# Folding the output weight early and spreading its projection over the last half batches of a cross attention kernel

## The chip, the cores and the metric

One core of a Trainium2 chip runs the whole program. The metric is the device time of one execution in microseconds. The engines are TensorE (PE; PEld is its weight load), VectorE (DVE), ScalarE (ACT), GpSimd (POOL) and SyncE (SP), which here only issues DMAs. PE accumulates in eight banks of PSUM; everything else lies in SBUF or, as scratch, in DRAM.

## What is computed

16 sequences of 112 queries attend to 375 context tokens each. There are 32 query heads and 8 key and value heads of width 32; all in float32.

```python
lin = lambda x, W, A, B: x @ W + 2.0 * (x @ A @ B)      # A, B: rank 16
q = lin(x, Wq, Aq, Bq)                                  # 1792 rows x 1024
k, v = lin(ctx, Wk, Ak, Bk), lin(ctx, Wv, Av, Bv)       # 6000 rows x 256
p = softmax(q @ k.T / sqrt(32))                         # per head, 4 query heads share one k, v
out = x + lin(p @ v, Wo, Ao, Bo)
```

## The kernel before

Each weight is folded once: W + 2AB is built block by block, one block being 128 rows of 1024. PE makes the product (`fold`, L706: two matmuls of 512 columns), DVE adds the raw weight (`block_sum`, L1149), ACT rounds the sum to a high part (`block_hi`, L976), and DVE (even blocks) or POOL (odd blocks) subtracts for the low part (`block_lo`, L1169; `pool_lo`, L637). Before a weight's first block its factor A is loaded, copied four times by DVE (`ab_place`, L1127), turned by PE (`turn_a`, L696, eight transposes) and split by ACT and DVE (`ab_hi`, L965; `ab_lo`, L1134). A product of split numbers is three matmuls (`mm3`, L689: L691, L692 and L693).

The query phase goes over 4 groups of 4 sequences. A group has 8 chunks (`q_chunk`, L741), called (g, c) here, of 8 k steps with three matmuls of 448 columns; ACT and DVE drain a chunk (`q_hi`, `q_lo`) and SP stores each pair of chunks (`store_q`, L490; two DMAs) to a scratch. ACT may overwrite a pair's buffer when the store of the pair two before has landed. A chunk needs the drain of the chunk two before. SP issues its DMAs in one written order: ahead of group 1 these are the first context (1.5 MB), then Ao in eight small loads and Bo in four (L435, L444), then the x of group 2 (L470).

The loop then takes one sequence ("batch") per step, in two halves of 4 key heads. A half of batch b holds the score matmuls of b (S, 12 of them, each followed by ACT's exponential and, from the fifth on, one of POOL's eight sums), the maxima of batch b+1 (N, 16 matmuls on two banks, each reduced by DVE, L1268; M turns them), the values or keys of later batches (V, T, K), and at the end the product with the values (P, 24 matmuls, L897) and the denominators (8, L932). `half_order` (L82) lays these out for every engine alike: the dense pieces stand in a row and set the clock with their `COST`, and each item of `PLAN` is put in where its due time, a share of the half, has come. `run_steps` (L390) says which kinds each half has.

The output weight comes last. Its factor is turned ahead of batch 0, where the second score matmul waits for it (L868). Its eight blocks are folded in the second half of batch 14 and the first half of batch 15 (W). Tile 0 of the output (14 tiles of 128 rows, each 2 x 8 x 3 matmuls of 512 columns, `o_piece`, L923) follows the blocks (O, in both halves of batch 15), tile 1 comes in the last half (Z). A tile's input is loaded from a scratch with its inverse denominators (`load_attn`, L563: one DMA and four of `load_inv`), multiplied by DVE (`normalise`, L1288), rounded by ACT (`split`, L1083) and split by DVE (L1294); DVE adds the residual (`add_residual`, L1299) and ACT stores the tile. Tiles 2 to 13 run behind the loop (`tile`, L942). Ahead of the loop ACT waits for all stores of queries (L1097), since the buffers of the output weight overlay theirs.

## Time and profile before

| | us |
|---|---|
| median of 3 runs (1038.49 to 1043.4) | 1040.0 |
| the profiled execution | 1043.98 |
| its span, first to last instruction | 1042.1 |
| PE busy in the span | 972.3 |
| DVE / ACT / POOL busy | 583.6 / 433.5 / 320.1 |

PE is busy when a matmul is in flight; busy is not the same as fast, since the granted clock has two levels (1.2 and 2.4 GHz), and the profile gives the mean granted share (PEclk) of a stretch. An idle time is put down to the instruction that ended it.

### The profile page before, as it was taken

The page shows a single profiled execution, that of the slowest core. Times are in us where ns is not written, and L with a number is a line of the kernel's source. Part 1 is how long each engine was busy: PE and PEld are TensorE (multiplying, and loading weights), DVE is VectorE, ACT ScalarE, POOL GpSimd, SP SyncE. Part 2 cuts the span into 40 slices and gives each one's busy share as a digit, 9 for nine tenths or more (in the row PEclk, how much of TensorE's full clock was granted, in tenths as well). Part 3 has the DMA queues.
Part 4 walks back from the last instruction along what each step waited for, and adds up shares of the span by engine and source line. Part 5 has one row for each costly group of instructions (what it writes and reads, how often), then busy time and mean ns, then how long its engine had stood idle before and what let it go on. Part 6 is the DMA issues. An engine that isn't in the chain of part 4 may idle for free.

```text
span 1042.1 us, 15943 instructions
## 1 busy us (share of the span) xinstructions
PE 972.3 (93%) x5904; PEld 802.1 (77%) x5904; DVE 583.6 (56%) x1005; ACT 433.5 (42%) x843; POOL 320.1 (31%) x276
## 2 busy tenths in 40 slices
PE   6989999977999999999999999999999767989998
PEld 4879999966887887887887877877878534768886
DVE  5661312257577676676677677667667643334321
ACT  3341211223555555555565565555655433201000
POOL 1201000000354354453453553553543545300000
PEclk9999999989899999999999999999999767989999
DMA  6739422643143443444344344245253442477652
GB/s 188 233 92 249 150 97 86 170 101 103 48 111 84 101 111 92 94 111 106 80 110 111 75 111 120 65 112 127 58 123 76 112 130 57 128 222 203 202 158 81
DMA packets 106004, 124.73 MB, mean 120 GB/s; under 512 B 30048, under 2 KB 89568, under 8 KB 105936
## 3 DMA queue, kind: packets, MB, share of 16 engines
q1 hardware_dynamic: 102076, 110.16, 41.3%
q10 hardware_dynamic: 3860, 13.67, 3.6%
q8 instruction: 42, 0.69, 0.3%
q14 instruction: 26, 0.21, 0.1%
HBM read 87.59 MB, written 29.82 MB: 113 GB/s over the span
## 4 chain that ended last, share of the span: by engine, by line
PE 74%; DVE 12%; DMA 5%; ACT 3%; issue 3%; SPq 1%; POOL 0%; ACTq 0%; DVEq 0%; POOLq 0%
PE ps L691 10%; PE ps L692 10%; PE ps L693 10%; PE ps L882 8%; PE ps L897 8%; PE ps L870 7%; PE ps L831 5%; PE ps L833 4%; PE ps L835 4%; PE ps L776 4%; DVE maxima L1268 4%; DVE k_stack L1197 3%; DMA q_scratch<-q_out_lo 3%; PE ps L932 2%; DMA out_dram<-residual 1%
## 5 line engine op out<-in xcount | busy, mean ns | idle before, releaser
L1268 DVE TENSOR_REDUCE maxima<-ps 112x1 f32<-112x375 f32 x512 | 269.2, 542 | 79.8 <-PE ps L882 71.2
L1060 ACT ACTIVATE probs<-ps 125x448 f32<-125x448 f32 x384 | 207.9, 543 | 170.1 <-PE ps L870 169.1
L671 POOL TENSOR_TENSOR prob_sum<-probs 125x448 f32<-125x448 f32 x128 | 146.0, 1156 | 343.4 <-ACT probs L1060 341.9
L882 PE MATMUL ps<-k_stack,q_stack 96*112 96x376 f32 x512 | 185.7, 363 | 21.9 <-DVE maxima L1268 20.3
L870 PE MATMUL ps<-q_stack,k_stack 97*125 97x448 f32 x384 | 146.8, 383 | 12.1 <-DVE a_stack_o L1146 4.3
L677 POOL TENSOR_TENSOR prob_sum<-prob_sum,probs 125x448 f32<-125x448 f32 x128 | 147.4, 1159 | 26.4 <-ACT probs L1060 24.9
L882 PEld LDWEIGHTS ps<-k_stack,q_stack 96*112 96x112 f32 x512 | 92.0, 180 | 46.1 <-DVE maxima L1268 42.0
L831 PE MATMUL ps<-wv_hi,ct_hi 128*125 128x256 f32 x384 | 112.6, 293 | 5.2 <-DVE k_stack L1197 5.2
L833 PE MATMUL ps<-wv_lo,ct_hi 128*125 128x256 f32 x384 | 109.4, 285 | 0.0
L835 PE MATMUL ps<-wv_hi,ct_lo 128*125 128x256 f32 x384 | 109.4, 285 | 0.0
L1191 DVE TENSOR_TENSOR ct_lo<-ps,ct_hi 128x375 fp32r<-128x375 f32 x128 | 70.2, 548 | 55.3 <-ACT ct_hi L997 55.3
L691 PE MATMUL ps<-xt_hi,wq_hi 128*128 128x448 f32 x256 | 97.4, 381 | 1.1 <-DVE wq_lo L1175 0.8
L693 PE MATMUL ps<-xt_hi,wq_lo 128*128 128x448 f32 x256 | 93.9, 367 | 0.0
L692 PE MATMUL ps<-xt_lo,wq_hi 128*128 128x448 f32 x256 | 93.9, 367 | 0.0
L691 PE MATMUL ps<-wo_hi,attn_hi 128*128 128x512 f32 x224 | 89.3, 399 | 3.9 <-DVE attn_lo L1296 3.9
L1197 DVE TENSOR_TENSOR k_stack<-ps,k_stack 32x376 fp32r<-32x376 f32 x128 | 70.0, 547 | 39.7 <-ACT k_stack L1003 36.7
L691 PE MATMUL ps<-ct_hi,wk_hi 128*128 128x376 f32 x256 | 90.7, 354 | 0.3 <-DVE ct_lo L1191 0.3
L693 PE MATMUL ps<-wo_hi,attn_lo 128*128 128x512 f32 x224 | 88.7, 396 | 0.0
L692 PE MATMUL ps<-wo_lo,attn_hi 128*128 128x512 f32 x224 | 88.7, 396 | 0.0
L897 PE MATMUL ps<-probs,v 125*32 125x448 f32 x768 | 82.6, 565 | 5.0 <-ACT probs L1060 4.9
L831 PEld LDWEIGHTS ps<-wv_hi,ct_hi 128*125 128x125 f32 x384 | 73.7, 192 | 17.0 <-DVE k_stack L1197 15.7
L692 PE MATMUL ps<-ct_lo,wk_hi 128*128 128x376 f32 x256 | 86.2, 337 | 0.0
(80 smaller groups left out, 1436.4 us busy)
## 6 DMA issues: line engine op xcount, KB each, us to landing
ctx_in<-in_ctx_dram SPq DMA_DIRECT2D x16, 1344.0 KB
q_stack<-q_scratch SPq DMA_DIRECT2D x96, 224.0 KB, 4.2
x_in<-in_x_dram SPq DMA_DIRECT2D x8, 896.0 KB, 8.7
q_scratch<-q_out_hi SPq DMA_DIRECT2D x16, 448.0 KB, 2.8
q_scratch<-q_out_lo SPq DMA_DIRECT2D x16, 448.0 KB, 3.7
attn_scratch<-attn SPq DMA_DIRECT2D x32, 224.0 KB, 4.1
attn_rows<-attn_scratch SPq DMA_DIRECT2D x14, 512.0 KB, 4.8
inv_tile<-inv_scratch SPq DMA_DIRECT2D x56, 128.0 KB, 5.1
```

Source lines behind the costliest of these rows:

```text
L677: pool.tensor_tensor(prob_sum[:, j, :], prob_sum[:, j, :], probs[:, 2, j, :], ALU.add).then_inc(psum_added, 1)
L691: pe.matmul(dst, l_hi, r_hi, start=start, stop=False)
L692: pe.matmul(dst, l_hi, r_lo, start=False, stop=False)
L693: return pe.matmul(dst, l_lo, r_hi, start=False, stop=stop)
L831: pe.matmul(dst, ct_hi[:, k, rows], wv_hi[:, k, :], start=(k == 0 and i != 1), stop=False, skip_group_check=True)
L833: pe.matmul(dst, ct_hi[:, k, rows], wv_lo[:, k, :], start=False, stop=False, skip_group_check=True)
L835: mm = pe.matmul(dst, ct_lo[:, k, rows], wv_hi[:, k, :], start=False, stop=(k == KC - 1), skip_group_check=True)
L870: pe.matmul(ps[0:TR, score_bank(i), 0:QH], kst[cur][0:STM, g, c * TR:(c + 1) * TR], qst[cur][0:STM, g, :], start=True, stop=True).then_inc ...
L882: mm = pe.matmul(ps[0:NQ, NAT + i % 2, 0:NTE], qst[nxt][0:STK, g, rr * NQ:(rr + 1) * NQ], kst[nxt][0:STK, g, :], start=True, stop=True)
L897: mm = pe.matmul(ps[HD * j:HD * (j + 1), CTX, 0:QH], v_sb[cur][:, c, g * HD:(g + 1) * HD], probs[:, c, j, :], start=(c == 0), stop=(c == T ...
L1060: act.activation(probs[:, c, j, :], ps[0:TR, score_bank(i), 0:QH], ACT.Exp, scale=SM).then_inc(exp_done, 1)
L1268: dve.tensor_reduce(maxima[:, h, i:i + 1], ps[0:NQ, NAT + i % 2, 0:NT], AX.X, ALU.max).then_inc(max_done, 1)
```

## The change

The output weight is folded in the query phase: its factor is turned in chunk (1, 2), and one block is folded in every second chunk from (1, 4) to (3, 2). The blocks use the staging buffers of the other weights; the high part overwrites the raw block, the low part the sum, and SP stores both to a new scratch in DRAM. The two halves of the weight's columns come back in batches 13 (left) and 14 (right). Six pieces of 24 matmuls each, one half of a tile's columns, stand in the last three half batches: the left halves of tiles 0 and 1, the right halves of tiles 0 and 1, then both halves of tile 2. Tiles 3 to 13 follow the loop. X is a tile's normalisation and Y its split. SP takes over the last denominators and the store of tiles 0 and 1, and ACT's wait for the stored queries is gone. Loops over registers are written out. Below is the core of the diff; the rest places buffers and renames arguments.

```diff
+EARLY = [(0, 0, VA), (1, 0, VB), (0, 1, TURN), (1, 1, VA), (2, 0, VB), (2, 1, TURN)]
+EARLY_TILES = 3
+LAST_PIECE = [2, 3, 5]
...
+O_TURN = (1, 2)
+O_FOLDS = {(1, 4): 0, (1, 6): 1, (2, 0): 2, (2, 2): 3, (2, 4): 4, (2, 6): 5, (3, 0): 6, (3, 2): 7}
+WO_KEEP = 7
...
-        "W": 2 * BANK, "O": 6 * BANK, "Z": 3 * BANK}
...
+EXTRA = {"U": [("X", 0, 0.35), ("Y", 0, 0.5)], "O0": [("X", 1, 0.25), ("Y", 1, 0.3)],
+         "O1": [("X", 2, 0.2), ("Y", 2, 0.6)], "O2": [("X", 3, 0.2), ("Y", 3, 0.45)]}
...
-    for name, first in (("W0", 0), ("W1", 4), ("W2", 8)):
-        if name in has:
-            for n in range(first, first + 4 if name != "W2" else KC + OLAG):
...
+    for n in range(HALVES + 1):
+        if f"O{n}" in has:
+            dense += [("O", p, k) for p in (2 * n, 2 * n + 1) for k in range(KC)]
...
-                return wo_hi[:, n, :], wo_lo[:, n, :]
+                return raw1[n % 2][:, :].bitcast(F32R), wsum1[n % 2][:, :].bitcast(F32R)
...
-            wo_factors()
...
-            step(B // 2 - 2, 1, (full[0], full[1] - {"C"}))
-            step(B // 2 - 1, 0, ({"A", "D", "V", "N"}, {"A", "D", "G", "N", "W0"}))
-            step(B // 2 - 1, 1, ({"A", "D", "W1"}, {"A", "D", "G", "W2"}))
+            step(B // 2 - 2, 1, (full[0] | {"L"}, (full[1] | {"L"}) - {"C"}))
+            step(B // 2 - 1, 0, ({"A", "D", "V", "N", "U"}, {"A", "D", "G", "N", "O0"}))
+            step(B // 2 - 1, 1, ({"A", "D", "O1"}, {"A", "D", "G", "O2"}))
...
+            return LAST_PIECE[t] + 1 if t < EARLY_TILES else 2 * t + 2
...
+                if w == W_O and n >= 2:
+                    sp.wait_ge(wo_stored[n % 2], 32 * (n // 2))
+                elif g >= 2:
                     sp.wait_ge(w_summed, g - 1)
...
+            def store_wo(n):
+                wait_lo(sp, QKV_BLOCKS + n)
+                for hl, t in enumerate((raw1, wsum1)):
+                    sp.dma_start(wo_scr[hl, n, :, :], t[n % 2][:, :]).then_inc(wo_stored[n % 2], 16)
+
+            def rows_q(g, n):
+                if (g, 2 * n) in O_FOLDS:
+                    block = O_FOLDS[g, 2 * n]
+                    store_wo(block)
+                    if block + 2 < KC:
+                        load_raw(W_O, block + 2)
+                store_q(g, n)
...
-            with sp.Fori(1, GROUPS - 1) as g:
+            for n in range(2):
+                load_raw(W_O, n)
+            for g in range(1, GROUPS - 1):
                 next_x(g)
                 for n in range(QS):
-                    store_q(g, n)
+                    rows_q(g, n)
             for n in range(QS - 1):
-                store_q(GROUPS - 1, n)
+                rows_q(GROUPS - 1, n)
...
+            def load_left(k):
+
+                for hl in range(2):
+                    to = wo0[hl][:, k, :] if k < WO_KEEP else wo0_end[hl][:, :]
+                    sp.dma_start(to.bitcast(F32), wo_scr[hl, k, :, 0:BANK]).then_inc(wo0_in, 16)
...
+            def load_right(hl):
+
+                for n in range(KC // 2):
+                    sp.dma_start(wo1[hl][:, 2 * n:2 * n + 2, :].bitcast(F32),
+                                 wo_scr[hl, 2 * n:2 * n + 2, :, BANK:H].rearrange("k p n -> p k n")
+                                 ).then_inc(wo1_in[n], 16)
...
-                    if "W0" in has[h]:
-                        load_attn(0, 0)
-                    if "W1" in has[h]:
-                        sp.wait_ge(st_done, NS * 2 * (B - 1))
-                        load_attn(0, 1)
-                        load_residual(sp, 0, 1)
+                    if "U" in has[h]:
+                        load_attn(0)
+                        sp.wait_ge(k_done, 2 * B)
+                        load_right(0)
...
-                        elif kind == "W" and i + 1 in range(2, KC):
-                            load_raw(W_O, i + 1)
-                        elif kind == "Z" and (i, k) == (0, 0):
-                            load_attn(1, 0)
+                        elif kind == "S" and i % 3 == 2 and "L" in has[h]:
+                            sp.wait_ge(st_done, NS * (2 * b + h) + i + 1)
+                            load_left(h * KC // 2 + i // 3)
+                        elif kind == "S" and i == 0 and "O0" in has[h]:
+                            sp.wait_ge(v_done, 2 * B)
+                            load_attn(1)
+                            load_residual(sp, 0)
+                            load_right(1)
+                            load_attn(2)
+                        elif kind == "S" and i == NS - 1 and "O0" in has[h]:
+                            sp.wait_ge(st_done, NS * 2 * (B - 1))
+                            load_residual(sp, 1)
+                        elif kind == "S" and i == 1 and "O1" in has[h]:
+                            load_attn(3)
+                        elif kind == "S" and i == 1 and "O2" in has[h]:
+                            for t in range(2):
+                                store_tile(sp, t)
+                                load_residual(sp, t + 2)
+                            load_attn(4)
...
+            run_steps(sp, step, second_queries)
             store_attn(B - 1, 1)
-            sp.wait_ge(st_done, NS * 2 * B)
-            load_residual(sp, 0, 0)
-            for h in range(HALVES):
-                sp.wait_ge(attn_stored[h], 16 * B)
-            sp.wait_ge(inv_stored, 16 * (B - 1))
-            with sp.Fori(2, OT // 2 - 1) as pair:
-                for par in range(2):
-                    load_attn(pair, par)
-            load_attn(OT // 2 - 1, 0)
-            sp.wait_ge(inv_stored, 16 * B)
-            load_attn(OT // 2 - 1, 1)
+            store_den(sp, 2 * B - 1, B - 1, 1)
+            load_attn(5)
+            load_attn(6)
+            sp.wait_ge(den_stored, 16 * 2 * B)
+            load_den(sp, B - 1)
+            load_attn(7)
+            store_inv(sp, B - 1)
+            for t in range(8, OT):
+                load_attn(t)
...
-            for n in range(1, KC, 2):
-                pool_lo(0, n)
+            for w in (0, W_O):
+                for n in range(1, KC, 2):
+                    pool_lo(w, n)
             wait_qkv(pool)
+            for par in range(2):
+                pool.wait_ge(wo_stored[par], 32 * KC // 2)
...
                 for c in range(2 * RH):
-                    q_chunk(g, c)
...
+                    if (g, c) == O_TURN:
+                        q_chunk(g, c, {KC // 2: lambda: turn_a(W_O, FOLD)})
+                    elif (g, c) in O_FOLDS:
+                        q_chunk(g, c, {KC // 2: lambda n=O_FOLDS[g, c]: fold(W_O, n, FOLD)})
+                    else:
+                        q_chunk(g, c)
+                if g < GROUPS - 1:
+                    pe.wait_ge(q_lo_set, g * 2 * RH + 2 * RH - 1)
...
-                            if i == S_IN_DEN[0] and isinstance(n, int) and n == 0:
-                                pe.wait_ge(a_lo, W_O + 1)
...
                         elif kind == "O":
-                            if i == 0:
...
+                            t, side, bank = EARLY[i]
+                            if k == 0:
+                                pe.wait_ge(at_lo_set, t + 1)
+                                if i < 2:
+                                    pe.wait_ge(v_set, 2 * B)
+                                    pe.wait_ge(wo0_in, 2 * KC * 16)
+                                elif i == 2:
+                                    pe.wait_ge(k_lo_set, NKV * B)
+                                else:
+                                    pe.wait_ge(o_added, i - 2)
+                            if i == 2 and k % 2 == 0:
+                                pe.wait_ge(wo1_in[k // 2], 32)
+                            mm = o_piece(t % 2, side, k, bank)
                             if k == KC - 1:
...
                 for m in range(2):
-                    if isinstance(pair, int) and par == 0:
+                    if t == EARLY_TILES:
+                        pe.wait_ge(o_added, 2 * t + m - 2)
+                    elif t == EARLY_TILES + 1:
                         pe.wait_ge(attn_set, 2 * B)
                         pe.wait_ge(den_copied, 2 * B)
                     else:
                         pe.wait_ge(o_added, 2 * t + m - 3)
                     for k in range(KC):
-                        mm = o_piece(par, m, k, OUT[par])
...
+            for t in range(EARLY_TILES, OT):
+                tile(t)
...
+                    if (g, c) == O_TURN:
+                        ab_hi(W_O, FOLD)
+                    if (g, c) in O_FOLDS:
+                        block_hi(W_O, O_FOLDS[g, c])
...
-            for par in range(2):
-                act.wait_ge(q_stored[par], GROUPS * QS // 2 * 32)
-            run_steps(act, step, lambda: None, wo_factors)
+                if t >= 2:
+                    act.wait_ge(o_done, added(t - 2))
+                if t == 1:
+                    act.wait_ge(v_done, 2 * B)
+                act.activation(at_hi[t % 2][:, :, :], at_raw[t % 2][:, :, :], ACT.Copy).then_inc(at_hi_set, 1)
+
+            run_steps(act, step, lambda: None)
...
-            store_den(act, 2 * B - 1, B - 1, 1)
-            split(1, 1)
...
-            act.wait_ge(inv_set, B - 1)
-            load_den(act, B - 1)
-            store_inv(act, B - 1)
...
-                    load_residual(act, pair, par)
-            for par in range(2):
-                store_tile(OT // 2 - 1, par)
+            for t in range(EARLY_TILES + 1, OT):
+                split(t)
+                store_tile(act, t - 2)
+                load_residual(act, t)
...
+                if w == W_O and n >= 2:
+                    dve.wait_ge(wo_stored[n % 2], 32 * (n // 2))
...
+                    if (g, c) == O_TURN:
+                        ab_lo(W_O, FOLD)
+                    if (g, c) in O_FOLDS:
+                        block_sum(W_O, O_FOLDS[g, c], FOLD)
+                        block_lo(W_O, O_FOLDS[g, c])
                     q_lo(g, c)
-                for k in range(KC):
-                    x_lo(g + 1, k)
-                q_lo(g, 2 * RH - 1)
-            for c in range(2 * RH - 1):
-                q_lo(GROUPS - 1, c)
+                    if (g, c) == (1, 0):
+                        ab_place(W_O)
...
-            ab_place(W_O)
...
-                        elif kind == "W":
-                            block_sum(W_O, i, FOLD_O)
-                            if i % 2 == 1:
...
+                        elif kind == "X":
+                            normalise(i)
+                        elif kind == "Y":
+                            split(i)
+                        elif kind == "S" and i == 2 and "O1" in has[h]:
+                            add_residual(1)
+                        elif kind == "O" and k == KC - 1 and i != 1:
+                            add_residual(i)
...
+            run_steps(dve, step, lambda: None)
+            copy_attn(B - 1, 2 * B - 1, 1)
+            normalise(EARLY_TILES + 1)
+            split(EARLY_TILES + 1)
+            for t in range(EARLY_TILES, OT):
+                if t + 2 < OT:
...
-            invert(B - 1)
...
+                    add_residual(2 * t + m)
+                if t + 2 < OT:
+                    split(t + 2)
+                if t == EARLY_TILES:
+                    invert(B - 1)
```

## Rows read from the trace of the kernel before

**Rows 1.** By stage: length; PE, PEld, DVE, ACT, POOL busy (count); PEclk, DMA share, GB/s.

```profile
105.00:155.00 50.00, 50.00 (x270) 46.03 (x269) 11.83 (x20) 10.65 (x20) 0.00 (x0) 1.00 0.40 128
...
800.50:817.80 17.30, 17.30 (x138) 14.60 (x134) 9.26 (x17) 8.07 (x16) 8.99 (x8) 1.00 0.29 69
817.80:848.30 30.50, 17.92 (x74) 9.71 (x70) 21.31 (x26) 11.72 (x19) 14.56 (x10) 0.61 0.43 111
848.30:878.10 29.80, 19.34 (x81) 11.20 (x77) 13.40 (x10) 11.25 (x18) 15.50 (x10) 0.77 0.38 97
878.10:899.90 21.80, 21.80 (x118) 16.16 (x115) 4.20 (x4) 7.92 (x14) 10.11 (x8) 1.00 0.42 109
899.90:926.50 26.60, 22.74 (x99) 18.29 (x99) 9.23 (x12) 2.66 (x3) 0.00 (x0) 0.98 0.62 193
926.50:1038.30 111.80, 111.71 (x480) 91.96 (x480) 35.60 (x40) 9.54 (x9) 0.00 (x0) 0.98 0.58 173
```

**Rows 2.** PE's timeline, 817 to 848 us: start, length, form, and in brackets idle before.

```profile
839.22 0.66 PE L882 MATMUL ps<-k_stack,q_stack 96*112 96x376 f32 x1 [7.74 <-DVE maxima L1268]
```

**Rows 3.** The chain that ended last, in order of time (start us, us, what): prices.

```profile
59.53 0.64 DVE a_dup L1131 x4
...
60.30 1.06 PE ps L701 x8
...
220.87 0.31 PE ps L882
...
222.55 0.18 PE ps L882
...
1037.78 0.23 PE ps L692
```

**Rows 4.** ACT's timeline in group 1 of the query phase: drains of chunks (1, 1), (1, 2).

```profile
84.40 0.55 ACT L991 ACTIVATE q_out_hi<-ps 128x448 fp32r<-128x448 f32 x1 [4.32 <-PE ps L693]
89.27 0.54 ACT L991 ACTIVATE q_out_hi<-ps 128x448 fp32r<-128x448 f32 x1 [4.32 <-PE ps L693]
```

**Rows 5.** The loads of a_in for Ao (78 to 105 us): issue, first and last start, landing.

```profile
L435 SPq DMA_DIRECT2D a_in<-in_L_xattn_Ao_dram x8: 317/435/698, 82.3 to 86.1; - x8
...
DMA to landing us min/median/max: 7.1/7.8/8.3
```

**Rows 6.** Waits, 200 to 262 us: who for whom, us in total, times, longest.

```profile
ACT k_stack L1003 <- DMA q_scratch<-q_out_lo: 10.2, 1, 10.2
...
PE ps L831 <- DVE k_stack L1197: 5.2, 1, 5.2
...
PE ps L870 <- DVE a_stack_o L1146: 4.3, 1, 4.3
```

**Rows 7.** The page's DMA issues: KB each and median us to landing.

```profile
q_scratch<-q_out_lo SPq DMA_DIRECT2D x16, 448.0 KB, 3.7
```

**Rows 8.** The chain that ended last again: landings, first maxima, ACT's copy of a tile.

```profile
90.54 12.29 DMA q_scratch<-q_out_lo
...
203.26 8.99 DMA q_scratch<-q_out_lo
...
217.06 0.62 PE ps L882
...
836.40 1.06 ACT attn_hi L1087
```

**Rows 9.** SP's queue: last query loads ahead of batch 14, the load of tile 2.

```profile
800.19 2.25 SPq L523 DMA_DIRECT2D q_stack<-q_scratch  x3
...
880.01 0.62 SPq L572 DMA_DIRECT2D attn_rows<-attn_scratch  x1
```

**Rows 10.** DVE's timeline: two normalisations in the loop's last halves.

```profile
833.00 3.36 DVE L1291 TENSOR_TENSOR attn_rows<-attn_rows,inv_tile 128x1024 f32<-128x1024 f32 x1
...
886.52 1.33 DVE L1291 TENSOR_TENSOR attn_rows<-attn_rows,inv_tile 128x1024 f32<-128x1024 f32 x1 [4.52 <-DMA inv_tile<-inv_scratch]
```

**Rows 11.** POOL's timeline: the operation under the first of them.

```profile
832.54 2.74 POOL L641 TENSOR_TENSOR wo_lo<-w_sum_o,wo_hi 128x1024 fp32r<-128x1024 f32 x1 [0.55 <-ACT wo_hi L980]
```

More of the change, by code:

```diff
@@ L106, in half_order @@
     plan = [item for item in PLAN if need[item[0]] in has]
+    plan = sorted(plan + [item for name in EXTRA if name in has for item in EXTRA[name]], key=lambda item: item[2])
     order, at = [], 0
@@ L199, in xattn_kernel @@
         ctx_in, at = place("ctx_in", [TR, TC, H], F32, r_cin)
-        wo_hi, at = place("wo_hi", [P, KC, H], F32R, r_kv)
-        wo_lo, at = place("wo_lo", [P, KC, H], F32R, r_ct)
-        assert at <= r_ks
+        wo1, at = [None, None], r_kv
+        for hl in range(2):
+            wo1[hl], at = place(f"wo_right{hl}", [P, KC, BANK], F32R, at)
+        assert at <= r_ct
+        wo0, wo0_end = [None, None], [None, None]
+        for hl in range(2):
+            wo0_end[hl], at = place(f"wo_left_end{hl}", [P, BANK], F32R, r_ct + hl * KC * QG * NQ * 4 + KC * NTE * 4)
+            assert at <= r_ct + (hl + 1) * KC * QG * NQ * 4
+        at = r_x
+        for hl in range(2):
+            wo0[hl], at = place(f"wo_left{hl}", [P, WO_KEEP, BANK], F32R, at)
+        assert at <= top[0]
         kst, v_sb = [None, None], [None, None]
@@ L317, in xattn_kernel @@
         attn_stored = [sem("attn_stored0"), sem("attn_stored1")]
+        wo_stored = [sem("wo_stored0"), sem("wo_stored1")]
+        wo0_in = sem("wo_left_in")
+        wo1_in = [sem(f"wo_right_in{n}") for n in range(KC // 2)]
         at_in = [sem("at_in0"), sem("at_in1")]
@@ L678, in step @@
                                                ).then_inc(psum_added, 1)
-                        elif kind == "W" and lo_by_pool(QKV_BLOCKS + i):
-                            pool_lo(W_O, i)
-            run_steps(pool, step, lambda: None, lambda: None)
+            run_steps(pool, step, lambda: None)
         @block.tensor
@@ L1024, in _ @@
             q_hi(0, 7)
-            with act.Fori(1, GROUPS - 1) as g:
+            for g in range(1, GROUPS):
                 for c in range(2 * RH - 1):
+                    if (g, c) == O_TURN:
+                        ab_hi(W_O, FOLD)
+                    if (g, c) in O_FOLDS:
+                        block_hi(W_O, O_FOLDS[g, c])
                     q_hi(g, c)
-                for k in range(KC):
-                    x_hi(g + 1, k)
-                q_hi(g, 2 * RH - 1)
-            for c in range(2 * RH - 1):
-                q_hi(GROUPS - 1, c)
+                if g < GROUPS - 1:
+                    for k in range(KC):
+                        x_hi(g + 1, k)
+                    q_hi(g, 2 * RH - 1)
             for k in range(KC):
@@ L1308, in wo_factors @@
-            def wo_factors():
-                ab_lo(W_O, CTX)
-            run_steps(dve, step, lambda: None, wo_factors)
-            copy_attn(B - 1, 2 * B - 1, 1)
-            add_residual(0, 0)
-            normalise(1, 1)
-            add_residual(0, 1)
-            split(1, 1)
-            invert(B - 1)
-            with dve.Fori(1, OT // 2 - 1) as pair:
-                for par in range(2):
-                    normalise(pair + 1, par)
-                    add_residual(pair, par)
-                    split(pair + 1, par)
@@ L1323, in _, with add_residual @@
-            for par in range(2):
-                add_residual(OT // 2 - 1, par)
+            def add_residual(piece):
+                if piece < len(EARLY):
+                    t, m, bank = EARLY[piece]
+                else:
+                    t, m = piece // 2, piece % 2
+                    bank = OUT[t % 2] + m
+                dve.wait_ge(res_in[t % 2], 16 * (t // 2 + 1))
+                dve.wait_ge(o_done, piece + 1)
+                part = res[t % 2][:, m * BANK:(m + 1) * BANK]
+                dve.tensor_tensor(part, ps[:, bank, :], part, ALU.add).then_inc(o_added, 1)
```

195 lines of the change are left out of this document (65 added, 130 removed).

## The prediction, made before the change was built

> **What bounds the kernel now.** I read the windows by stage first, to see where TensorE (PE) stands still, then the waits there. In the query phase PE is never idle [rows 1]: whatever is put in there lengthens it. The loop's half batch that still projects values, 800.5 to 817.8, is full too. The next two half batches, 817.8 to 848.3 and 848.3 to 878.1, are not: PE works 17.9 of 30.5 us and 19.3 of 29.8 us, at a mean granted clock of 0.61 and 0.77. The reader is to see in the PE rows [rows 2] that these are stops for VectorE (DVE) and ScalarE (ACT), up to 7.7 us long, where the folding of the output weight stands in front of the maxima and exponentials. The last half batch, 878.1 to 899.9, is full and carries 72 output matmuls; the tail after it has 3.9 us without PE work in its first 26.6 us [rows 1] and then one matmul every 0.23 us [rows 3].
>
> **The change, part by part.** All sums are made against the profiled execution, 1043.98 us.
>
> 1. Folding moved into the query phase. 16 fold matmuls of 512 columns at 0.23 us are 3.7 us, and the eight transposes of the small factor are 1.06 us [rows 3]; PE has no gap there [rows 1], so 4.8 us go on the path. DVE, ACT and GpSimd (POOL) do the rest of the fold beside it: DVE and ACT are busy 11.8 and 10.7 of 50 us [rows 1].
>
> The transposes bring a wait. They stand after the fifth of eight k steps of chunk (1, 2). Chunk (1, 1) has ended when ACT drains it at 84.40; a chunk takes 4.87 us [rows 4], so PE is there at 84.4 + 5/8 x 4.87 = 87.4. They need the copies of `a_in`, which this change puts on DVE right behind chunk (1, 0). The eight loads of `a_in` are issued where they were, the last at 86.1, and land after 7.1 to 8.3 us, 7.8 in the middle [rows 5]: 93.9, and 0.6 us of copies [rows 3] make 94.5. PE stops for 7.1 us. DVE waits in order, so chunk (1, 1)'s low part is late as well, but only PE's chunk (1, 3) wants it, behind the same stop. After such a stop PE runs at the lower of its two levels: after the 5.2 us stop near 215 the same matmul takes 0.31 us at 220.9 and 0.18 us at 222.6 [rows 3, 6], so about 7 us went by at half speed, 3.5 us lost. I take 3.5 us (bounds 0 and 4). Part 1 is 3.7 + 1.1 + 7.1 + 3.5 = **+15.4 us**, bounds +5 and +19.
>
> The Trainium skill (DMA: Bandwidth & Descriptors, Anatomy of one DMA) gives a load some 2.0 us fixed plus bytes over bandwidth, fitted on loads that GpSimd issues; by that the last `a_in` is there at 88.1, PE stops for 1.3 us, and the sum is about 9 us lower. The rows have 7.1 us at least, behind a 1.5 MB context load on the same queue, and I go by them.
>
> SyncE (SP) now also stores each folded block, waits for that store to land, loads the block after next and only then stores the queries. Eight issues at about 0.44 us [rows 5] are 3.5 us; two chunks with a fold take 2 x 4.87 + 0.46 = 10.2 us. A landing of up to 6.7 us is hidden. The 448 KB store takes 3.7 us [rows 7]; 512 KB twice lies nearer to that than to the 12.3 us of the one crowded store at 90.5 [rows 8]. I take nothing; the other end is the slow rival.
>
> 2. The step into the loop. ACT no longer waits for all query stores before the first keys: it stood 10.2 us [rows 6], the store landing at 203.26 + 8.99 = 212.25 [rows 8]. What is late next is the SBUF copy of the keys, which queues behind that store; about 213 for the first maxima matmul, which ran at 217.06 [rows 8]. That is -4.1 us, and -1 us for a shorter slow stretch (bounds 0 and 3.5). The wait of 4.3 us for `a_stack_o` [rows 6] goes altogether, with up to 3.5 us of slow clock after it (I take 2.5, the stop being nearly as long as the 5.2) and the 1.1 us of transposes. Part 2 is -5.1 - 7.9 = **-13.0 us**, bounds -6 and -16.
>
> 3. First half of batch 14, full before. The load of tile 0 goes out when SP is through the last query loads, 800.19 + 2.25 = 802.4 [rows 9]. Such a load took from 880.01 to DVE's start at 886.52, 6.5 us [rows 9, 10]: 809. DVE comes to the normalisation at 35% of the half, near 806.6, and the maxima queue behind it; PE may run two maxima matmuls ahead. The operation takes 1.33 us, or 3.36 us when POOL is in the middle of one [rows 10, 11]. I take **+3.5 us** with some slow clock, bounds 0 and +6.
>
> By the Trainium skill (SBUF — State Buffer, SBUF: two separate sides) DVE and GpSimd hold their shared port for a whole instruction, so DVE waits at most for the POOL operation in flight: the 3.36 us stand behind a 2.74 us operation and agree [rows 11]. With the full 3.36 us in its place each of parts 3 and 4 would cost about 1 us more than I take.
>
> 4. Second half of batch 14. Take the full last half batch, 21.8 us with 72 output matmuls [rows 1]; 24 fewer at 0.23 leave 16.3 us for 48. With 16 maxima matmuls at 0.18 [rows 3] this half needs 19.2 us of PE. Tile 1's load goes out 2 us into it (as at 880.01 in the half begun at 878.1), lands at 8.4 us, and DVE reaches it at 25%, after 5 to 6 us. Behind it stand the later maxima, the split, and piece 1, the left half of tile 1. Normalisation (some 2.4 us, between the 1.33 and the 3.36), ACT's copy (1.06 us [rows 8]) and a split as long as the quick normalisation end at 8.4 + 2.4 + 1.1 + 1.3 = 13.2 us; PE would want piece 1 at about 9, with half of its matmuls done: 4.2 us, with a second short stop for the late maxima 4.7 us, and 2 us of slow clock. 30.5 becomes 25.9, **-4.6 us**, bounds -11 and -1.
>
> 5. Batch 15. Both halves now hold 48 output matmuls and no maxima, so a late DVE stops nobody: 16.3 us, and 0.7 us because POOL's eight sums end about when PE wants them. 29.8 becomes 17.0, **-12.8 us** (bounds -13.5 and -8); 21.8 becomes 17.0, **-4.8 us** (bounds -5.5 and 0). The weight comes from the scratch in batches 13 and 14, with SP's and the DMA engines' spare time as cover (share 0.29 to 0.43 [rows 1]); without it the pieces would wait some 5 us.
>
> 6. Tail. 26.6 + 111.8 us and 3.8 us of last store, 142.2, for 12 tiles. Now 11 tiles of 48 x 0.23 = 11.04 us are 121.4, with the store 125.2: **-17.0 us**, bounds -18.6 and -12. The stop of 3.9 us goes because SP, not DVE's order, now waits for the last denominators.
>
> Sum: 15.4 - 13.0 + 3.5 - 4.6 - 12.8 - 4.8 - 17.0 = -33.3 us, 1010.7 in the profiled execution's terms. That execution lies 4.0 us above the median of 1040.0, so **1007 us**. Taking all bounds together, the ends would be far off; with most parts near their values and one or two at an end, 990 to 1024.
>
> **The rivals.**
> - *DVE's waits are hidden* (tiles 0 and 1 land in time). Against it: the 6.5 us of such a load. Parts 3 and 4 give 3.5 + 6.7 us back: 997.
> - *`a_in` lands early*, as a store in a quiet queue does, after 3.7 us [rows 7]: at 89.8, PE stops 3.0 us instead of 7.1 and perhaps keeps its clock, 999 to 1003. For it speaks the skill's fixed cost named above; against it all eight rows of that load.
> - *The half batches of batch 15 stay at the loop's length.* If exponentials and POOL's sums set the pace, 17.0 becomes some 19.2 twice: 1011.
> - *Slower: SP's wait for each block's store.* Its price is the landing beyond 6.7 us, on six blocks. At the 12.3 us of the crowded store [rows 8] that is 5.6 x 6 = 34 us, with slow clock after each stop up to 55: 1041 to 1062. The gain of 33 us is used up from a landing of 12.2 us, or 8.7 us if every stop costs 3.5 us of clock. Against it: away from 80 to 105 the DMA engines are busy 0.40 of the time [rows 1].
> - That the change doesn't do what it says has no place here: every piece moved has its own line.
>
> **How the numbers follow.** Forecast 0.50; hidden waits 0.18; early `a_in` 0.07; batch 15 at loop pace 0.12; SP's wait 0.13, of which 0.05 stays below 1035, 0.04 within 0.5% of 1040 and 0.04 above. A change of 0.5%, 5.2 us, is about what a measurement of this kernel can tell from none. Faster by more: 0.92; within: 0.04; slower: 0.04. The likeliest case's own range is 998 to 1016.
>
> **What would show it.** In the profile after: PE waiting some 7 us for DVE's `a_dup` near 87; the first key copies on ACT near 206 and no wait for `a_stack`; DVE waiting for `inv_tile` in batch 14; batch 15's halves near 17 us at clock 1.0; a tail near 125 us. Query stores waiting on SP, or PE on `q_out_lo` in groups 1 to 3, would make the forecast wrong to the slow side; no stop near 87 to the fast side.

## The result, and the profile after

The changed kernel takes **1013.3 us** (median of 4, 1009.0 to 1014.2) against 1041.0 us for the kernel before beside it: ratio 0.972, 95% interval 0.969 to 0.976. Forecast were 1007 us in 990 to 1024. The profiled execution is one of 1013.9 us, with a span of 1011.9 us, 30.2 us less than before.

The stages first, against [rows 1]. After its bounds each row gives PE, PEld, DVE, ACT and POOL busy, then the granted clock, the DMA share and GB/s.

```profile
80.00:105.00 25.00, 17.78 (x80) 16.11 (x79) 6.08 (x10) 3.72 (x5) 0.00 (x0) 0.80 1.01 243
105.00:155.00 50.00, 50.00 (x262) 45.81 (x261) 18.91 (x24) 13.13 (x22) 4.79 (x2) 1.00 0.71 237
...
804.40:826.80 22.40, 19.02 (x136) 15.99 (x134) 12.08 (x20) 9.14 (x17) 9.01 (x8) 0.92 0.66 191
826.80:854.00 27.20, 22.56 (x110) 16.32 (x110) 12.56 (x22) 8.29 (x15) 9.63 (x8) 0.87 0.67 204
854.00:871.00 17.00, 17.00 (x93) 12.01 (x93) 5.39 (x7) 8.04 (x14) 9.74 (x8) 1.00 0.29 77
871.00:888.10 17.10, 17.10 (x97) 12.11 (x93) 6.06 (x6) 8.05 (x14) 9.89 (x8) 1.00 0.66 200
888.10:914.70 26.60, 26.60 (x118) 22.00 (x119) 11.59 (x12) 3.73 (x4) 0.00 (x0) 1.00 0.83 233
914.70:1008.10 93.40, 93.30 (x412) 76.96 (x410) 27.14 (x30) 7.43 (x7) 0.00 (x0) 1.00 0.50 156
```

The reader is to see that the halves of batch 15 and the start of the tail are now all PE at full clock, that the halves of batch 14 are not (0.92 and 0.87), and that a hole of 7.2 us has opened in the query phase, in a stretch where the DMA engines are fully busy (share 1.01). PE's own rows there, with the wait in brackets:

```profile
88.24 0.37 PE L755 MATMUL ps<-xt_hi,wq_lo 128*128 128x448 f32 x1
95.84 1.94 PE L763 MATMUL ps<-ident,a_dup 128*128 128x128 f32 x8 [7.22 <-DVE a_dup L1168]
97.43 0.72 PE L753 MATMUL ps<-xt_hi,wq_hi 128*128 128x448 f32 x1
97.95 0.57 PE L754 MATMUL ps<-xt_lo,wq_hi 128*128 128x448 f32 x1
...
101.09 0.37 PE L754 MATMUL ps<-xt_lo,wq_hi 128*128 128x448 f32 x1
```

The chain over the same stretch names the cause, the last of the eight 8 KB loads of `a_in`:

```profile
87.11 7.92 DMA a_in<-in_L_xattn_Ao_dram
95.06 0.64 DVE a_dup L1168 x4
```

At the step into the loop the chain shows the first key matmul, PE's stop, and the first maxima matmul of batch 0; SP's rows below show what was issued ahead of the copy of the keys (L577) that PE, by the order of the program, waits for there; run 7 tests it.

```profile
216.81 0.41 PE ps L753
...
225.67 4.35 issue
230.01 0.40 PE ps L944
```

```profile
216.49 0.82 SPq L505 DMA_DIRECT2D ctx_in<-in_ctx_dram  x2
218.12 0.38 SPq L523 DMA_DIRECT2D q_scratch<-q_out_hi  x1
218.55 1.94 SPq L523 DMA_DIRECT2D q_scratch<-q_out_lo  x1
223.23 4.66 SPq L577 DMA_DIRECT2D k_stack<-k_stack  x2
```

In batch 14 the normalisations of tiles 0 and 1 on DVE (first fence) and the maxima matmuls on PE that stood behind them (second):

```profile
814.49 1.35 DVE L1330 TENSOR_TENSOR attn_rows<-attn_rows,inv_tile 128x1024 f32<-128x1024 f32 x1 [3.12 <-DMA inv_tile<-inv_scratch]
...
836.77 1.22 DVE L1330 TENSOR_TENSOR attn_rows<-attn_rows,inv_tile 128x1024 f32<-128x1024 f32 x1 [3.85 <-DMA inv_tile<-inv_scratch]
```

```profile
816.35 0.43 PE L944 MATMUL ps<-k_stack,q_stack 96*112 96x376 f32 x1 [3.38 <-DVE maxima L1312]
...
838.51 0.65 PE L944 MATMUL ps<-k_stack,q_stack 96*112 96x376 f32 x1 [3.32 <-DVE maxima L1312]
```

Where the 30.2 us come from (spans of the two profiled executions; the query phase ends with the first key matmul, 201.50 before and 216.81 after):

| stage | forecast | measured |
|---|---|---|
| query phase | +15.4 | +15.3 |
| first key matmul to batch 14, the step into the loop with it | -13.0 | -11.4 |
| batch 14, first half | +3.5 | +5.1 |
| batch 14, second half | -4.6 | -3.3 |
| batch 15, first half | -12.8 | -12.8 |
| batch 15, second half | -4.8 | -4.7 |
| tail | -17.0 | -18.4 |
| sum | -33.3 | -30.2 |

### The profile page after: what moved, and what is told of

Read it like the earlier page. It is cut to its first block, busy times and chain, and to the rows that moved or that the text cites. A ratio compares the mean times of both kernels' runs of the same rounds, so it can differ in the third digit from the quotient of the medians.

```text
span 1011.9 us, 15606 instructions
## 1 busy us (share of the span) xinstructions
PE 960.2 (95%) x5904; PEld 797.7 (79%) x5904; DVE 579.8 (57%) x1005; ACT 435.1 (43%) x843; POOL 319.1 (32%) x276
## 4 chain that ended last, share of the span: by engine, by line
PE 79%; DVE 10%; DMA 3%; ACT 3%; issue 3%; SPq 2%; POOL 0%; ACTq 0%; DVEq 0%; POOLq 0%
PE ps L753 12%; PE ps L754 11%; PE ps L755 11%; PE ps L944 8%; PE ps L959 7%; PE ps L932 7%; PE ps L895 5%; PE ps L897 4%; PE ps L838 4%; PE ps L899 4%; DVE maxima L1312 4%; DVE k_stack L1236 3%; PE ps L995 2%; DMA inv_tile<-inv_scratch 1%; PE ps L793 1%
## 5 line engine op out<-in xcount | busy, mean ns | idle before, releaser
L932 PE MATMUL ps<-q_stack,k_stack 97*125 97x448 f32 x384 | 144.0, 375 | 0.0
L755 PE MATMUL ps<-ct_hi,wk_lo 128*128 128x376 f32 x256 | 85.6, 334 | 0.0
L895 PEld LDWEIGHTS ps<-wv_hi,ct_hi 128*125 128x125 f32 x384 | 72.7, 189 | 11.5 <-DVE k_stack L1236 10.2
L1055 ACT ACTIVATE ct_hi<-ps 128x375 fp32r<-128x375 f32 x128 | 62.0, 484 | 40.2 <-PE ps L838 39.2
L959 PE MATMUL ps<-probs,v 125*32 125x448 f32 x768 | 78.8, 543 | 0.0
L897 PEld LDWEIGHTS ps<-wv_lo,ct_hi 128*125 128x125 f32 x384 | 72.8, 190 | 1.9
```

Source lines behind the costliest of these rows:

```text
L755: return pe.matmul(dst, l_lo, r_hi, start=False, stop=stop)
L895: pe.matmul(dst, ct_hi[:, k, rows], wv_hi[:, k, :], start=(k == 0 and i != 1), stop=False, skip_group_check=True)
L897: pe.matmul(dst, ct_hi[:, k, rows], wv_lo[:, k, :], start=False, stop=False, skip_group_check=True)
L932: pe.matmul(ps[0:TR, score_bank(i), 0:QH], kst[cur][0:STM, g, c * TR:(c + 1) * TR], qst[cur][0:STM, g, :], start=True, stop=True).then_inc ...
L959: mm = pe.matmul(ps[HD * j:HD * (j + 1), CTX, 0:QH], v_sb[cur][:, c, g * HD:(g + 1) * HD], probs[:, c, j, :], start=(c == 0), stop=(c == T ...
```

## The experiments

The theory: what the change loses is three waits for small transfers that stand behind big ones in SP's queue (`a_in`, the second copy of the first keys, the tile loads of batch 14). The rivals are, for each, that another wait stands right behind it, and for the whole, that SP's stores of the folded weight set the pace. Each ratio is against the kernel before on the run's own chip (1038.8 to 1040.2 us); runs 1 to 4, 5 to 8, and 9 and 10 shared one each. Run 5 is the changed kernel again.

**1. The small loads ahead of the context.** `load_ab(W_O)` goes in front of `load_ctx(0)`.

```
-            load_ctx(0)
             load_ab(W_O)
+            load_ctx(0)
```

> SP issues Ao and Bo ahead of the first context instead of behind it; nothing else changes. In the changed kernel (1013.3 us) the last load of Ao landed 7.9 us after its issue and PE stopped for 7.2 us at the transposes of the factor. Theory: the loads are late because 1.5 MB of context and the stores before it stand ahead of them on the queue. Then the eight loads land some 4 us after their issue, the last near 89, PE reaches the transposes at 88.6, the stop shrinks to about 1 us, its slow stretch goes, and the time falls by 8 to 10 us, to about 1004. Rival 1: such small pieces are slow by themselves, landing stays near 8 us; then only the 2.2 us of earlier issue are gained, 1009 to 1011. Rival 2: the stop comes back as a wait for the query stores behind the crowded queue, at chunk (1, 4) or (1, 6); then the time stays at 1010 to 1013.

Measured: 1014.4 us, 0.976 [0.973, 0.979]: no gain. The loads of `a_in` (first fence, the tile's own view) are quick now, with only one store of queries (0.9 MB) issued ahead of them, and PE no longer stops for them. But a new stop of 6.9 us has come four chunks later, at chunk (1, 6) (second, PE's waits from 80 to 205 us), and the chain (third) gives its cause: a store of queries.

```profile
DMA to landing us min/median/max: 1.6/1.9/2.5
```

```profile
PE ps L753 <- DVE q_out_lo L1224: 6.9, 1, 6.9
```

```profile
93.39 17.82 DMA q_scratch<-q_out_lo
111.24 0.55 ACT q_out_hi L1049
111.82 0.63 DVE q_out_lo L1224
```

That store took 17.8 us; ctx(0) (1.5 MB), two raw blocks of the weight (1 MB) and the next x (1.8 MB) had been issued ahead of it, and run 6 tests whether they are the reason. ACT may not overwrite the query buffer until the store lands. The price is the same, under another name: it is the second rival's mechanism, at a time 1.4 us above its range.

**2. The turn of Ao two chunks later**, all folds with it.

```
-O_TURN = (1, 2)
+O_TURN = (1, 4)
...
-                    if (g, c) == (1, 0):
+                    if (g, c) == (1, 2):
```

> The turn of the factor moves from chunk (1, 2) to (1, 4), DVE's copies from behind chunk (1, 0) to behind (1, 2), and each fold by two chunks, the last to (3, 4). All loads stay as they are issued. Theory: the 7.2 us stop and its slow stretch (together some 10 us) are the price of wanting Ao two chunks too early and nothing else; two chunks are 9.8 us, so there is no stop and the time falls to about 1003. Rival: without the stop ACT meets the late store of chunks (1, 0) and (1, 1), now behind another 1 MB of weight, and PE stops there for 3 to 4 us with a slow stretch; then 1008 to 1010.

Measured: 1009.4 us, 0.971 [0.969, 0.974]. The stop for `a_dup` is gone and a stop for the query store appears, shorter than in run 1 (PE's waits from 80 to 205 us):

```profile
PE ps L753 <- DVE q_out_lo L1224: 3.4, 1, 3.4
```

In the trace the query phase ends 4.8 us earlier (first key matmul at 211.99). The rival's time, not the theory's: waiting later for the same queue gives back part of it.

**3. The tile loads one half earlier**, tile 0 in batch 13's second half, tile 1 at the head of batch 14's second half.

```
+                    if "O0" in has[h]:
+                        sp.wait_ge(v_done, 2 * B)
+                        load_attn(1)
                     if "U" in has[h]:
-                        load_attn(0)
...
+                        elif kind == "S" and i == 0 and h == 1 and "L" in has[h]:
+                            load_attn(0)
                         elif kind == "S" and i == 0 and "O0" in has[h]:
-                            sp.wait_ge(v_done, 2 * B)
-                            load_attn(1)
```

> SP issues the load of tile 0 half a batch earlier (with the first scores of the second half of batch 13) and that of tile 1 at the head of the second half of batch 14 instead of behind its stores of denominators, some 5 us earlier. DVE's and ACT's order stays. Theory: the 22.4 and 27.2 us of the two halves of batch 14 come from DVE waiting 3.1 and 3.9 us for tile loads, with PE's stops and slow clock after them; the first half goes back to about 18 us, the second to 21 to 22, the time to about 1003 to 1005. Rival: DVE is simply full there (normalisation, split, maxima, with POOL on the shared port); then each half gains at most the wait of one maximum, 2 us in all, 1011.

Measured: 1002.9 us, 0.965 [0.962, 0.969]. Both normalisations start without a wait for a load, and batch 14 takes 18.4 and 23.8 us instead of 22.4 and 27.2 (DVE's rows, then the windows of its two halves):

```profile
806.48 1.21 DVE L1332 TENSOR_TENSOR attn_rows<-attn_rows,inv_tile 128x1024 f32<-128x1024 f32 x1
...
824.10 1.22 DVE L1332 TENSOR_TENSOR attn_rows<-attn_rows,inv_tile 128x1024 f32<-128x1024 f32 x1
```

```profile
799.60:818.00 18.40, 17.69 (x137) 14.47 (x134) 11.83 (x20) 9.02 (x17) 10.93 (x8) 1.00 0.62 178
818.00:841.80 23.80, 22.03 (x114) 16.08 (x111) 12.57 (x22) 8.32 (x16) 10.32 (x8) 0.93 0.79 232
```

So the two late loads cost 7.4 us of batch 14. The second half stays some 2 us above the 21 to 22 us that were expected: two stops for maxima, 1.4 and 0.4 us, are left in it, and its clock is 0.93. (The run's median lies 8.1 us under that of run 5 and 10.4 under the first measurement; what goes beyond 7.4 us stands, in the trace, in the query phase and just behind it, which this edit does not touch and which scatter by that much.)

**4. ACT's wait for all query stores put back** ahead of the loop, the one small part of the change undone.

```
+            for par in range(2):
+                act.wait_ge(q_stored[par], GROUPS * QS // 2 * 32)
             run_steps(act, step, lambda: None)
```

> ACT again waits for all stores of queries ahead of the loop, as in the kernel before; nothing else. Theory: this wait, not only the wait for the folded factor, was part of the step into the loop. In the changed kernel the first maxima matmul follows the first key matmul by 13.2 us; with the wait back the keys' copies start at about 227.6 instead of 221.2, the SBUF copy of the keys lands later, and the distance grows by 2 to 4 us: 1015 to 1018. Rival: the SBUF copy of the keys was queued behind the stores anyway, so that the wait costs nothing here: 1013, distance unchanged.

Measured: 1014.7 us, 0.977 [0.973, 0.982], by the time alone between the two forecasts. The trace is clearer: ACT stands 11.6 us for the last store, PE 6.5 us for the keys, and from the first key matmul (215.18) to the first maxima matmul it takes 16.9 us instead of 13.2 and 11.8 in the two traces of the changed kernel.

```profile
227.36 3.97 ACT L1061 ACTIVATE k_stack<-ps 32x376 fp32r<-32x376 f32 x8 [11.57 <-DMA q_scratch<-q_out_lo]
```

```profile
230.20 0.58 PE L895 MATMUL ps<-wv_hi,ct_hi 128*125 128x256 f32 x1 [6.51 <-DVE k_stack L1238]
...
232.08 0.63 PE L944 MATMUL ps<-k_stack,q_stack 96*112 96x376 f32 x1 [0.88 <-issue]
```

By this stretch dropping that wait is worth 3.7 to 5.1 us, as forecast (4.1 and 1). The time alone does not show it: 1014.7 us stand against 1013.3 and 1011.0 for the changed kernel, since this execution makes good 1.6 us in the query phase and 1.7 us in batch 14, where nothing was edited.

**5. The changed kernel again**, as the measure for runs 6 to 8.

> The changed kernel itself, nothing edited, run beside the three that follow and timed against the kernel before, so that they have it on their own chip. Both theories: 1010 to 1014 us. In its trace the last drain of ct_lo ends the query phase between 215 and 217.5 us, and from the first key matmul to the first maxima matmul of batch 0 it takes 11.4 to 13.2 us, which is how far two traces of kernels with the same code in this stretch lie apart.

Measured: 1011.0 us, 0.972 [0.968, 0.977]. The query phase ends at the same place (first key matmul at 216.87), PE's stop before the first maxima matmul is 2.9 us instead of 4.35.

**6. SP's order in the query phase alone**: ctx(0) in the last group, the raw blocks behind a query store.

```
-            load_ctx(0)
             load_ab(W_O)
-            for n in range(2):
-                load_raw(W_O, n)
...
                     rows_q(g, n)
+                    if g == 1 and n == 0:
+                        for m in range(2):
+                            load_raw(W_O, m)
             for n in range(QS - 1):
                 rows_q(GROUPS - 1, n)
+                if n == 0:
+                    load_ctx(0)
```

> SP's order alone is changed in the query phase: ctx(0) (1.5 MB) is loaded in the last query group, where it is used, and the first two blocks of the raw output weight (1 MB) behind the first query store of group 1. Theory (the stop at the turn of Ao, and the later wait for a query store that came in its place when Ao was moved or the turn put off, are one queue: bytes that nobody needs yet lie ahead of a load or a store that PE waits for): the loads of Ao land in 1.6 to 2.5 us, PE has no wait of over 1.5 us between 80 and 205 us and no slow clock there, the last drain of ct_lo comes at 207 to 209 us instead of 217, and the time is 1002 to 1006 us. Rival (the stretch lacks bandwidth as a whole, and whatever is put last becomes the next wait, ctx(0) itself or the load of x): a wait of 3 to 7 us at another place, the phase ends at 212 to 215 us, 1008 to 1012 us.

Measured: 1003.6 us, 0.964 [0.958, 0.969], 7.4 us below run 5. The last drain comes at 205.8 us, 11.3 us earlier, and the only wait left from 80 to 205 us is this one:

```profile
PE ps L765 <- DVE a_dup L1170: 0.5, 1, 0.5
```

What the folding costs by itself is counted from the drain of chunk (1, 1), since what lies ahead of it differs by some 2 us between executions. These are the drains in run 6 and in the changed kernel, to be set beside the 84.40 of [rows 4]:

```profile
83.50 0.55 ACT L1051 ACTIVATE q_out_hi<-ps 128x448 fp32r<-128x448 f32 x1 [4.26 <-PE ps L757]
```

```profile
85.61 0.55 ACT L1049 ACTIVATE q_out_hi<-ps 128x448 fp32r<-128x448 f32 x1 [4.26 <-PE ps L755]
```

From there to the first key matmul it is 117.1 us before (to 201.50), 122.2 in run 6 (to 205.70) and 131.2 in the changed kernel (to 216.81; 131.0 in run 5). So the folding costs 5.1 us, about its 4.8 us of matmuls, and the queue cost 9. Some 4 of these 9 are given back at the next places: the first maxima matmul comes 13.4 us behind the first key matmul, against 11.8 in run 5, after a stop of 4.5 us for the key copy, and with PE at half clock behind it the first value product follows after 52.4 us, against 49.7.

```profile
219.08 0.62 PE L946 MATMUL ps<-k_stack,q_stack 96*112 96x376 f32 x1 [4.53 <-issue]
```

**7. The key copies ahead of the last query store.**

```
             load_ctx(1)
-            store_q(GROUPS - 1, QS - 1)
 
             def second_queries():
+                store_q(GROUPS - 1, QS - 1)
                 sp.wait_ge(q_done, GROUPS * 2 * RH)
```

> On SP the last store of queries (0.9 MB) is issued after the second copies of the first keys, not before them. Theory (the first maxima matmul waits for that copy, which lies behind ctx(1) and the store on SP's queue): from the first key matmul to the first maxima matmul 9.5 to 10.5 us instead of 11.4 to 13.2, PE's stop there under 1 us instead of 2.5 to 4.3; the time is 1.5 to 3.5 us under the changed kernel's. Rival (the copy is late because its source is: ACT's drains of the keys, 219.7 to 226.9 us, set it): the stop stays at 2.5 us or more and the time is the changed kernel's within 1 us.

Measured: 1009.4 us, 0.970 [0.965, 0.975]: 1.7 us below run 5, which the intervals do not tell from nothing. In the trace the stop is gone, and 9.3 us lie between the first key and the first maxima matmul:

```profile
223.66 0.40 PE L944 MATMUL ps<-k_stack,q_stack 96*112 96x376 f32 x1 [0.48 <-issue]
```

From there to the first value product this trace takes 52.5 us, that of run 5 49.7; its clock is 0.91 from 243 to 258 us, with no long stop ahead of it. So the copy's place in the queue is shown as the cause of the stop; what removing it is worth alone is not settled.

**8. Edits 3, 6 and 7 together.**

> Three edits together: the tile loads of the output projection issued one half earlier (as in the run that did it alone, 1002.95 us), the order of SP in the query phase, and the second key copies ahead of the last query store. Theory (the three stops are at three places of the chain and add): 1013.3 - 10 - 8.5 - 2.5 = 992 us, between 989 and 995. Rival (they share the queue, so that one's gain is another's loss): 996 to 1000 us.

Measured: **990.7 us** (990.0 to 991.2), 0.952 [0.948, 0.956]: 20.3 us under the changed kernel, run 5. Alone the three edits gave 8.1, 7.4 and 1.7 us against run 5, 17.2 in all. The three waits add; that one's gain is another's loss, as the rival had it, would have shown as less than the sum. The clock line of the profile page (tenths, 40 slices) has no dip left:

```profile
PEclk9999999999999999999999999999999999999999
```

**9. Each folded block stored twice**, for the slower rival. The waits for the stores count both.

```
...
                     sp.dma_start(wo_scr[hl, n, :, :], t[n % 2][:, :]).then_inc(wo_stored[n % 2], 16)
+                    sp.dma_start(wo_scr2[hl, n, :, :], t[n % 2][:, :]).then_inc(wo_stored[n % 2], 16)
...
```

> The changed kernel, with each folded block of the output weight stored a second time, into a second scratch that nobody reads; SP, DVE and POOL wait for both copies. It takes the margin of the slower rival: SP's wait for each block's store, with the query stores and x loads queued behind it, at twice the bytes. Theory (there is room: a store lands in 2.6 to 8.9 us, and blocks come 11 us apart): the stores land in 4 to 13 us, PE stops for 0 to 3 us in all between 105 and 205 us, and the time is that of the changed kernel plus 0 to 4 us. Slower rival (SP was near its edge): the landing passes 12 us, ACT's or DVE's wait for a store or a raw block stops PE for 5 us or more, in several chunks, and the clock falls with it: plus 8 to 20 us.

Measured: 1016.4 us, 0.978 [0.976, 0.981]; the changed kernel had 0.972 twice, so the second store costs some 6 us, by medians 3 to 5. The store's longest landing is 12.2 us. PE has one stop that the changed kernel does not have, 2.5 us at 168.28, and the chain that leads to it is the slower rival's: block stores that land late, SP's raw loads and then the query store held up behind them, ACT, which may not overwrite the query buffer, and DVE behind ACT, so that the low part of x is late:

```profile
136.27 12.22 DMA wo_scratch<-w_sum_qkv
...
154.53 5.49 DMA wo_scratch<-w_sum_qkv
...
162.26 4.21 DMA q_scratch<-q_out_lo
...
166.50 0.55 ACT q_out_hi L1051
...
167.70 0.54 DVE xt_lo L1221
...
168.28 0.60 PE ps L795 x4
```

Twice the bytes cost about as much as the theory allowed (0 to 4 us) or a little more, and less than the rival said (8 to 20). The change as it is has no stop of PE from 105 to 205 us, so there is a margin, but at twice the bytes it is used up. What lies behind it is cheap: one stop of 2.5 us.

**10. The same second store with SP's new order.**

> The same second store, in the kernel with SP's order changed in the query phase (1003.6 us there). It tells the bytes from the order: if the queue has room once ctx(0) and the first raw blocks are out of the way, plus 0 to 4 us against 1003.6; if the bytes of this stretch are the limit, ctx(0), which now lies among the last stores, is late as well and the phase ends 5 us or more after 205.8 us.

Measured: 1010.2 us, 0.973 [0.970, 0.976], 6.6 us over run 6, and the phase ends at 214.8. With 8 MB more the bytes do limit: DMA share 1.01 from 180 to 205 us (0.64 in run 6), and PE stops at 151.44, 162.74 and 209.06 us for 3.1, 1.5 and 3.1 us. The last is a stop for the low part of the context (`ct_lo`), but the context itself is there: DVE is held up by ACT, which stands 8.1 us for a query store of 13.1 us.

```profile
194.20 13.13 DMA q_scratch<-q_out_lo
...
207.35 0.55 ACT q_out_hi L1053
...
209.06 0.54 PE ps L842 x3
```

So the phase ends late as the second theory said, though by a store and not by ctx(0). Order alone helped in run 6, where the DMA engines had idle time (share 0.68 to 0.81 from 80 to 205 us). With the second store it still gives 6.2 us (1010.2 against 1016.4), but the longest stores land late in either order (12.2 and 13.1 us).

## Why the prediction was right, and where its terms were off

The direction and the mechanism came out as forecast, and the time lies in the range and in the likeliest case's own range. The distance from 1007 (1006.7 before it was rounded) is 6.6 us and has two halves of about the same size. The terms summed to 3.1 us too much gain. The other 3.4 us is the last step: the profiled execution of before lay 4.0 us above its median and I took all of it off, while that of after lies 0.6 us above its own. How far one execution stands from the median is no property that the next kernel inherits: in runs 1 to 10 the profiled execution lies anywhere from 3.2 us below its median to 1.5 us above.

1. **Query phase**, +15.4 forecast, +15.3 measured, by two misses that cancel. The stop is right (7.1 us, measured 7.22), the slow clock too dear: the transposes took 1.94 instead of 1.06 us and eight matmuls came 0.37 us apart instead of 0.20, together 2.3 us, not 3.5. About 1.2 us had been lost already when chunk (1, 1) was drained (85.61 against 84.40 in [rows 4]). The trace gives the cause: from 70 to 75 us, ahead of all that the change moves, the granted clock was 0.66 in this execution and 1.00 in that of before (rows in the last section). This scatters from execution to execution (first key matmul at 214.3 to 216.9 us in the five runs with this order of SP and the early turn that store each block once), so that the two misses cancel is luck. That PE is never idle in the query phase was read from rows that show 105 to 155 us only; it holds, but for 0.4 us, from 80 to 105 us as well, where the first of the work was put; ahead of 80 us PE has some 14 us of waits, on which no term rests. The rows of [rows 5] were the right price for `a_in`. By the Trainium skill (DMA: Bandwidth & Descriptors, Anatomy of one DMA), some 2.0 us fixed for a load that GpSimd issues, the stop would by estimate have been 1.3 us: the runs show both. The same eight loads, issued by SP, land in 1.9 us (median) in run 1, with one query store ahead of them, which agrees, and in 8.0 us behind the context.

2. **The step into the loop**, -13.0 forecast, -11.4. The wait for `a_stack_o` [rows 6] is gone and ACT starts the keys at once. The first maxima matmul was put 11.5 us behind the first key matmul (213 against 201.5); it came after 13.2 us in this trace and after 11.8 us in the repeat. So the step that failed is small: the key copy, which I had behind the last query store, is late by as much as SP's queue happens to be. In run 7, with the copy ahead of that store, it took 9.3 us.

3. **Batch 14, first half**, +3.5 forecast, +5.1. The mis-sized term is the tile's load: 6.5 us from [rows 9, 10], measured 8.8 (issued at 805.69, DVE's start at 814.49). Behind the load that I took the price from stood a small store and the load of the next tile, at a DMA share of 0.86; here the right halves of the weight, 2 MB, were issued straight behind it and share the engines, at 1.10. Run 3 holds the comparison: its tile 0 has 1 MB of left halves straight behind it and the slowest of its denominators lands 6.0 us after its issue, its tile 1 has only small transfers next to it and needs 4.2 us; in the changed kernel it is 6.2 and 5.7 us.

4. **Batch 14, second half**, -4.6 forecast, -3.3. The same term, 8.1 us instead of 6.5 (issued at 828.70, DVE's start at 836.77). Two stops of 3.3 and 1.3 us are there as described, and the clock is 0.87. Run 3 shows that both halves lose this to the loads alone.

5. **Batch 15**, 17.0 and 17.0 us forecast, 17.0 and 17.1 measured, PE without a gap. The rival of the loop's own length falls.

6. **Tail**, 125.2 us forecast, 123.8; the stop of 3.9 us is gone as said.

The slow normalisation that was costed as a bound (3.36 us, by POOL's operation in flight [rows 10, 11]) did not come: both took 1.2 to 1.4 us. The rival that `a_in` lands early would have been no gain either, as run 1 shows, since the query store is next on that queue. I had not seen that second wait; it could have been read from [rows 8], where a store took 12.3 us in just this stretch. The slower rival falls by the trace: the block stores land in 2.6 to 8.9 us, and from 105 to 205 us PE has no stop. It was priced too strictly, though. A landing above 6.7 us was said to cost PE its excess; landings of up to 8.9 us cost nothing, and run 9's 12.2 and 5.5 us one behind the other cost one stop of 2.5 us, where 34 us and more were forecast for six such landings.

## What to carry to other kernels

When work moves into a phase that feeds from one queue, that is from the DMAs that one engine issues in a written order, price each small load by the bytes that were issued ahead of it, and look for the second transfer behind the same bytes before you move the first: here moving the load or its user alone gained nothing or 2 to 4 us, moving the bytes that nobody needed yet gained 7 (run 6, against run 5). Then find the latest place where a big load may stand and put it there. Take a price from a row with the same neighbours on its queue, and leave one execution's distance from its median out of the sum.

## What the hardware did that I had not expected

The clock's answer to the same short stops is not the same each time. Ahead of all that the change moves, each of the twelve traces has two stops of PE near 68 and 70 us, of 1.5 and 0.5 us, at the transposes of x. In the changed kernel the second transposes took 0.98 us, at a granted clock of 0.66 from 70 to 75 us, so partly at the lower level; in run 3, behind the same stops, they took 0.57 us at 1.00 (PE's rows of the changed kernel, then of run 3):

```profile
68.46 0.60 PE L793 MATMUL ps<-ident,x_in 112*128 112x112 f32 x4 [1.49 <-DVE xt_lo L1219]
...
70.22 0.98 PE L793 MATMUL ps<-ident,x_in 112*128 112x112 f32 x4 [0.55 <-DVE xt_lo L1219]
```

```profile
68.71 0.60 PE L795 MATMUL ps<-ident,x_in 112*128 112x112 f32 x4 [1.48 <-DVE xt_lo L1221]
...
70.47 0.57 PE L795 MATMUL ps<-ident,x_in 112*128 112x112 f32 x4 [0.55 <-DVE xt_lo L1221]
```

Of the twelve, the changed kernel and runs 2 and 5 show 0.66 there, the other nine 1.00. What decides it no run shows. From the first maxima matmul to the first value product the eleven traces of the changed kernel and its variants take 49.7 to 52.5 us, while the steady loop behind it, up to the last value product ahead of batch 14, takes 520.0 to 520.2 us in all of them. The two traces of the changed kernel, 3.2 us apart in span, part by 3.0 us between the first key matmul and the first value product, where the stop for the key copy lies. That such stops make the scatter between executions in general is not shown; the version without long stops has the narrowest times, 990.0 to 991.2 us.
